# Attention on TensorE: scores from two rounded float32 parts in two 64-row halves, in place of three bfloat16 parts in the whole array

## The reference

```python
x = x + 0.5 * ffn(layernorm(x), ...)
# attention, 16 heads of 16, on y = layernorm(x)
Q = ((y @ W_dq) @ W_uq).reshape(4, 1024, 16, 16)
c = y @ W_dkv
K = (c @ W_uk).reshape(4, 1024, 16, 16)
V = (c @ W_uv).reshape(4, 1024, 16, 16)
scores = einsum('bqhd,bkhd->bhqk', Q, K) / sqrt(16)
attn = softmax(where(causal, scores, -inf))
x = x + einsum('bhqk,bkhd->bqhd', attn, V).reshape(4, 1024, 256) @ W_o
x = x + 0.5 * ffn(layernorm(x), ...)
```

## Time and profile before

| | us |
|---|---|
| median of 3 runs (1258.01 to 1261.18) | 1259.8 |
| span of the profiled execution, first to last instruction | 1263.3 |
| PE busy in it | 1066.7 |
| DVE busy | 829.9 |
| ACT busy | 666.1 |

### The profile page before, as it was taken

How to read it: one execution, slowest core, us unless ns; L and a number is a source line. 1 busy time by engine, 2 the same in 40 slices (tenths; PEclk the granted TensorE clock), 3 DMA queues, 4 the chain that set the end, 5 groups by cost and what they waited for, 6 DMA issues and landing times. The chain is left out here.

```text
span 1263.3 us, 22520 instructions
## 1 busy us (share of the span) xinstructions
PE 1066.7 (84%) x6988; PEld 642.3 (51%) x6988; DVE 829.9 (66%) x2536; ACT 666.1 (53%) x1668; POOL 384.3 (30%) x404
## 2 busy tenths in 40 slices
PE   3539999984988899999999999999859369999940
PEld 2328888872442244443444444444347258888840
DVE  6774444436867888888888888888037754444427
ACT  5605554542753376676777666667636315455520
POOL 6506777752002000000000000000048227777730
PEclk8559999995977699999999999999889759999985
DMA  9503333326756444444444444440057113333339
GB/s 301 186 9 93 101 105 105 102 84 216 201 200 142 59 60 61 61 61 60 61 61 60 60 61 61 61 60 11 10 189 239 58 38 94 104 102 104 105 118 331
DMA packets 109248, 132.53 MB, mean 105 GB/s; under 512 B 29968, under 2 KB 83664, under 8 KB 109136
## 3 DMA queue, kind: packets, MB, share of 16 engines
q1 hardware_dynamic: 91280, 89.65, 31.2%
q0 software_dynamic: 13632, 37.24, 9.3%
q10 hardware_dynamic: 4224, 4.19, 1.0%
HBM read 82.42 MB, written 48.23 MB: 103 GB/s over the span
## 5 line engine op out<-in xcount | busy, mean ns | idle before, releaser
L1415 ACT ACTIVATE stacks_rows_or_prob<-stacks_bank 128x512 f32<-128x512 f32 (+3 forms) x768 | 326.0, 494 | 144.1 <-PE stacks_bank L1347 118.9
L1429 DVE CUSTOM_DVE_ANT_0 stacks_bank<-stacks_bank,all_causal 128x128 f32<-128x128 f32 (+3 forms) x512 | 245.4, 504 | 33.7 <-PE stacks_bank L1318 30.2
L1432 DVE TENSOR_REDUCE t_maxp<-stacks_bank 128x1 f32<-128x512 f32 x256 | 175.5, 686 | 25.0 <-PE stacks_bank L1318 24.4
L1318 PE MATMUL stacks_bank<-stacks_kst,stacks_qst 96*128 96x512 bf16 (+2 forms) x528 | 160.3, 348 | 8.5 <-DVE t_maxp L1429 4.2
L1358 PE MATMUL stacks_bank<-stacks_rows_or_prob,stacks_turned_or_values 128*32 128x512 f32 (+3 forms) x1536 | 164.5, 500 | 3.0 <-ACT stacks_rows_or_prob L1415 1.1
L1344 PE MATMUL stacks_bank<-stacks_qst,stacks_kst 99*128 99x512 bf16 (+3 forms) x528 | 154.9, 335 | 2.5 <-ACT stacks_rows_or_prob L1415 1.9
L1296 POOL COPY stacks_turned_or_values<-stacks_values 128x512 f32<-128x512 f32 x16 | 9.8, 613 | 427.7 <-DMA stacks_kst<-qk_parts 286.5
L1318 PEld LDWEIGHTS stacks_bank<-stacks_kst,stacks_qst 96*128 96x128 bf16 x528 | 48.5, 98 | 126.9 <-DVE t_maxp L1429 66.6
L653 PE MATMUL be_psG<-b_w,be_xT 128*128 x426 | 112.8, 401 | 0.0
L653 PE MATMUL ae_psG<-a_w,ae_xT 128*128 x426 | 111.9, 398 | 0.0
L1347 PE MATMUL stacks_bank<-all_causal_t,all_ident_bf 128*128 128x128 bf16 x512 | 109.6, 221 | 0.0
(11 more groups left out here) (296 smaller groups left out, 1917.7 us busy)
## 6 DMA issues: line engine op xcount, KB each, us to landing
stacks_qst<-qk_parts SPq DMA_DIRECT2D x66, 128.0 KB, 4.9
stacks_kst<-qk_parts SPq DMA_DIRECT2D x66, 128.0 KB, 7.6
stacks_rows_or_prob<-y_rows SPq DMA_DIRECT2D x16, 512.0 KB, 6.1
s_yk<-y_rows SPq DMA_DIRECT2D x16, 512.0 KB, 9.4
stacks_parts_or_stacks<-qk_parts SPq DMA_DIRECT2D x60, 128.0 KB, 6.2
qk_parts<-stacks_parts_or_stacks SPq DMA_DIRECT2D x16, 384.0 KB, 2.6
qk_parts<-q_parts SPq DMA_DIRECT2D x16, 384.0 KB, 3.4
o_rows<-t_orow SPq DMA_DIRECT2D x32, 136.0 KB, 8.7
```

The lines of the kernel that those rows point to most:

```text
L1318: nc.tensor.matmul(psR[bank][:, 0:w], qst[slot][0:KROWS, h, i * P:(i + 1) * P], kst[slot][0:KROWS, h, k0:k0 + w], start=True, stop=True).t ...
L1415: nc.scalar.activation(prob[j % 2][:, h, a:(c + 1) * 512], psS[n % ST_BANKS][:, a - c * 512:512], ACT.Exp, scale=DK ** -0.5).then_inc(exp_ ...
L1429: ins = nc.vector.tensor_tensor_reduce(psR[bank][:, 0:w], psR[bank][:, 0:w], T.causal[:, 512 - w:512], 1.0, -BIG, ALU.add, ALU.max, maxp[: ...
L1432: ins = nc.vector.tensor_reduce(maxp[:, h, col:col + 1], psR[bank][:, 0:w], AX_X, ALU.max)
```

## The change

Q, K and the maxima are kept in two rounded float32 parts (F32R, fp32r) in place of three bfloat16 parts. Three products of parts remain (high times high, high times low, low times high), so a stack has 3 x 16 = 48 rows, 50 with the maxima. Even heads of a group lie in partitions 0 to 63 and odd heads in 64 to 127, so S and T of the two use different 64-row halves of the array; S and T are at least 256 columns wide now (a 128-column piece computes 256). The pieces of S alternate between the two halves, and T's heads do so too. The mask matmul stays as it is. The projections drop `take_high` and `middle`: the high part by ACT, the low one by one DVE subtraction. `split_max` has two operations, `load_max` four DMAs. The rows of ones are written for partitions 32 to 63 and 96 to 127 before the stacks load, and SP waits for that. `plan_step` gives each half a time of its own. The stores of parts grow from 384 to 512 KB each; a group's stack loads remain 12 of 128 KB.

```diff
-PARTS = 3
-Q_PARTS = (0, 0, 0, 1, 1, 2)
-K_PARTS = (0, 1, 2, 0, 1, 0)
+PARTS = 2
+Q_PARTS = (0, 0, 1)
+K_PARTS = (0, 1, 0)
 KROWS = len(Q_PARTS) * DK
 MROWS = KROWS + PARTS
+HALVES = 2
+HALF_ROWS = P // HALVES
+ROUNDED_COLS = 256
...
+    PAIRS = HG // HALVES
+    N_LOADS = HALVES * (len(Q_PARTS) + len(K_PARTS))
...
-        self.qst = [M.sb(f"qst{s}", [P, HG, S], BF16) for s in range(SLOTS - 1)] + [last[0]]
-        self.kst = [M.sb(f"kst{s}", [P, HG, S], BF16) for s in range(SLOTS - 1)] + [last[1]]
+        self.qst = [M.sb(f"qst{s}", [P, self.PAIRS, S], F32R) for s in range(SLOTS - 1)] + [last[0]]
+        self.kst = [M.sb(f"kst{s}", [P, self.PAIRS, S], F32R) for s in range(SLOTS - 1)] + [last[1]]
...
+    def rows(self, st, slot, h, n):
+
+        at = (h % HALVES) * HALF_ROWS
+        return st[slot][at:at + n, h // HALVES, :]
 
     def load(self, sp, g, slot):
         b, hg = g // self.GB, g % self.GB
         for kind, st, which in ((0, self.qst, Q_PARTS), (1, self.kst, K_PARTS)):
             for r, part in enumerate(which):
                 src = self.qk_dram[kind, part, bass.ds(hg * (HG * DK), HG * DK), bass.ds(b * S, S)]
-                sp.dma_start(st[slot][r * DK:(r + 1) * DK, :, :],
-                             src.rearrange("(h d) t -> d h t", d=DK)).then_inc(self.loaded[slot], 16)
+                by_half = src.rearrange("(c a d) t -> a d c t", a=HALVES, d=DK)
+                for a in range(HALVES):
+                    at = a * HALF_ROWS + r * DK
+                    sp.dma_start(st[slot][at:at + DK, :, :].bitcast(F32), by_half[a]).then_inc(self.loaded[slot], 16)
...
+                sp.wait_ge(Q.ones_ready, HALVES * (SLOTS - 1))
...
-                dve.wait_ge(mid_ready, c * NU + u + 1)
-                nc.vector.tensor_tensor(parts[b][:, u, 2, :], bank(c, u)[:], parts[b][:, u, 1, :], ALU.subtract).then_inc(low_ready, 1)
+                dve.wait_ge(high_ready, c * NU + u + 1)
+                nc.vector.tensor_tensor(parts[b][:, u, 1, :], bank(c, u)[:], parts[b][:, u, 0, :], ALU.subtract).then_inc(low_ready, 1)
...
-        def take_high(c, b, u):
-            pe.wait_ge(high_ready, c * NU + u + 1)
-            nc.tensor.matmul(bank(c, u)[:], T.minus_bf[:], parts[b][:, u, 0, :], start=False, stop=True,
-                             skip_group_check=True).then_inc(high_taken, 1)
...
-            take_high(c, b, 0)
+            up(c, b, 2)
             if more:
                 turn(c + 1, 1 - b)
-            take_high(c, b, 1)
-            up(c, b, 2)
             up(c, b, 3)
-            take_high(c, b, 2)
             Q.early_scores(pe, c, 1)
             if more:
                 latents(c + 1, 1 - b)
-            take_high(c, b, 3)
...
-        def middle(c, b, u):
-            act.wait_ge(high_taken, c * NU + u + 1)
-            nc.scalar.copy(parts[b][:, u, 1, :], bank(c, u)[:]).then_inc(mid_ready, 1)
...
-    for h in range(HG):
+    for pair in range(HG // HALVES):
         for i in range(QT):
             end = (i + 1) * P
-            units.append((h, i, 0, min(end, 512), i))
-            if end > 512:
-                units.append((h, i, 512, end - 512, i + QT // 2))
+            for k0 in range(0, end, 512):
+                for a in range(HALVES):
+                    units.append((pair * HALVES + a, i, k0, min(end - k0, 512), i + k0 * QT // (2 * 512)))
...
+            half = half_free[units[u][0] % HALVES] if kind == "s" else max(half_free)
...
+            can.append((max(t, half_free[h % HALVES], st_free[n_st % ST_BANKS], slot_free - 300), had_t / need_t, "t"))
...
-            t = start + w / 2.4
-            dve = max(dve, t + READER_LATENCY) + 64 + (w if kind == "s" else 900) * 1.04
+            end = start + max(w, ROUNDED_COLS) / 2.4
+            if kind == "s":
+                half_free[units[u][0] % HALVES] = end
+                t = start + ISSUE
+            else:
+                half_free = [end] * HALVES
+                t = end
...
-            t = start + (w + P * (max(c * 512, j * P) == j * P)) / 2.4
-            act = max(act, t + READER_LATENCY) + 100 + w * 0.833
+            end = start + max(w, ROUNDED_COLS) / 2.4
+            half_free[h % HALVES] = end
+            t = start + ISSUE
+            if max(c * 512, j * P) == j * P:
+                end = t = max(half_free) + P / 2.4
+                half_free = [end] * HALVES
...
-                sp.dma_start(qst[slot][KROWS + part:KROWS + part + 1, :, :], mparts[:, part, :]).then_inc(m_loaded, 16)
+            wait(sp, drained, max_at(g))
+            for a in range(HALVES):
+                at = a * HALF_ROWS + KROWS
+                rows = slice(a * (MROW // HALVES), (a + 1) * (MROW // HALVES))
+                for part in range(PARTS):
+                    sp.dma_start(qst[slot][at + part:at + part + 1, :, :].bitcast(F32),
+                                 mparts[rows, part, :].bitcast(F32)).then_inc(m_loaded, 16)
...
+    def ones(pool, s):
+
+        for a in range(HALVES):
+            rows = slice(a * HALF_ROWS + HALF_ROWS // 2, (a + 1) * HALF_ROWS)
+            Q.ones_chain.link(nc.gpsimd.memset(kst[s][rows, :, :].bitcast(F32), 1.0))
...
         wait(pe, drained, r + 1 - RING_BANKS)
-        nc.tensor.matmul(psR[bank][:, 0:w], qst[slot][0:KROWS, h, i * P:(i + 1) * P],
-                         kst[slot][0:KROWS, h, k0:k0 + w], start=True, stop=True).then_inc(filled, 1)
+        w = max(w, ROUNDED_COLS)
+        nc.tensor.matmul(psR[bank][:, 0:w], A.rows(qst, slot, h, KROWS)[:, i * P:(i + 1) * P],
+                         A.rows(kst, slot, h, KROWS)[:, k0:k0 + w], start=True, stop=True).then_inc(filled, 1)
 
...
+            wide = min(a, (c + 1) * 512 - ROUNDED_COLS)
             wait(pe, exp_done, g * ST + n + 1 - ST_BANKS)
-            ins = nc.tensor.matmul(ps, kst[k][0:MROWS, h, j * P:(j + 1) * P], qst[k][0:MROWS, h, a:(c + 1) * 512],
-                                   start=True, stop=a > j * P)
+            ins = nc.tensor.matmul(psS[n % ST_BANKS][:, wide - c * 512:512], A.rows(kst, k, h, MROWS)[:, j * P:(j + 1) * P],
+                                   A.rows(qst, k, h, MROWS)[:, wide:(c + 1) * 512], start=True, stop=a > j * P)
             if a == j * P:
                 ins = nc.tensor.matmul(ps[:, 0:P], T.ident_bf[:], T.causal_t[:], start=False, stop=True)
             ins.then_inc(st_done, 1)
...
-            wait(dve, m_loaded, g * (16 * PARTS))
-            nc.vector.tensor_scalar(neg[:], psR[bank][0:MROW, 0:P], -1.0, None, ALU.mult).then_inc(drained, 1)
-            dve.wait_ge(drained, r + 1)
-            link(nc.vector.tensor_copy(mparts[:, 0], neg[:]), g, 2)
-            link(nc.vector.tensor_tensor(mid[:], neg[:], mparts[:, 0], ALU.subtract), g, 3)
-            link(nc.vector.tensor_copy(mparts[:, 1], mid[:]), g, 4)
-            nc.vector.tensor_tensor(mparts[:, 2], mid[:], mparts[:, 1], ALU.subtract).then_inc(m_ready, 1)
+            wait(dve, m_loaded, g * M_LOADS)
+            turned = psR[bank][0:MROW, 0:P]
+            link(nc.vector.tensor_scalar(mparts[:, 0], turned, -1.0, None, ALU.mult), g, 2)
+            nc.vector.scalar_tensor_tensor(mparts[:, 1], turned, -1.0, mparts[:, 0], ALU.mult,
+                                           ALU.subtract).then_inc(drained, 1)
```

More of the change, by code:

```diff
@@ L1145, in plan_step @@
         if n_ring < len(ring):
-            can.append((max(t, ring_free[n_ring % RING_BANKS], joined if ring[n_ring][0] == "m" else 0.0), had_s / need_s, "r"))
+            kind, u = ring[n_ring][:2]
+            half = half_free[units[u][0] % HALVES] if kind == "s" else max(half_free)
+            can.append((max(t, half, ring_free[n_ring % RING_BANKS], joined if kind == "m" else 0.0), had_s / need_s, "r"))
         if n_st < len(st):
@@ L1303, in step @@
                     pool.wait_ge(stored, (Q.CH // 2) * (16 * Q.NU))
-                first.link(nc.gpsimd.memset(kst[SLOTS - 1][KROWS:MROWS, :, :], 1.0))
+                ones(pool, SLOTS - 1)
         def blank(s):
@@ L1426, in row_max @@
         h, i, k0, w, col = units[u]
+        half, pair = h % HALVES, h // HALVES
         dve.wait_ge(filled, r + 1)
@@ L1429, in row_max @@
             ins = nc.vector.tensor_tensor_reduce(psR[bank][:, 0:w], psR[bank][:, 0:w], T.causal[:, 512 - w:512], 1.0, -BIG,
[L1430 removed]
+                                                 ALU.add, ALU.max, maxp[:, half, pair, col:col + 1])
         else:
[L1432 removed]
+            ins = nc.vector.tensor_reduce(maxp[:, half, pair, col:col + 1], psR[bank][:, 0:w], AX_X, ALU.max)
         ins.then_inc(drained, 1)
```

79 lines of the change are left out of this document (39 added, 40 removed).

## The result

The changed kernel takes 1435.9 us (median of 4 runs, 1435.2 to 1436.0 for three of them and 1506.7 for the fourth, which lies outside the comparison) against 1258.9 us: a ratio of 1.142, interval 1.136 to 1.147. It is slower, by more than the 1370 that I forecast. The profiled execution spans 1433.9 us.

A forecast was written before the change was run, and what follows sets the result against it. PE was taken to set the 30.7 us step; streams -4.5 and row-mode changes +11.7 gave 37.9. Fifteen steps +108, the last +5, projections -4: 1259.8 + 109, written 1370 us, range 1280 to 1450.

The forecast's parts named there:

- the named mechanism: PE in the groups: changes between 64-row and 128-row matmuls cost gaps and operand reloads, 11.7 us a group.
- The streams: S and T on PE: 64-row halves side by side take 11.5 us in place of 16.0, gain 4.5 a group.
- the turns of PV and transposes: PE's 128-row work among 64-row S and T: PV reloads +1.2 us, turned maxima and outputs +0.9 us a group.
- The masks' turns: 32 masks a group between 64-row matmuls: 0.10 us out, 0.10 back, 0.10 reload each, +9.6 us a group.
- The step at full clock: One step of a group on PE at 2.4 GHz: 30.7 - 4.5 + 11.7 = 37.9 us, +7.2.
- rival 2: PE's clock falls to 1.2 GHz among the groups: about 56 us a group, about 1660 us in all; chance 0.27.
- third of the time: Milder case of the clock's fall: PE at 1.2 GHz a third of the time, about 1500 us.
- the halting pattern: PE's drains and loads between streams in the groups: the stop-and-go that lowered the clock earlier was said to persist.
- The last step: Last step of the groups, T alone: masked T find no S to pair with, partly covered by ACT's exponentials, +5 us.
- The projections: Projections: PE loses 32 `take_high`, ACT 32 copies, stores grow by a third; -4 us in all.
- Maxima split, memsets, load order: DVE's shorter maxima split, POOL's memsets of ones, and the maxima's and stacks' loads: no effect on the time.
- Rival 1: Gaps on PE are cheap and reloads hide, so DVE binds at 26.7 us a step: about 1194 us; chance 0.18.

The follow-up runs named there:

- b_mask64: Kernel before, each mask matmul replaced by two 64-row matmuls in partitions 0 to 63, other matmuls as they were; 1355.4 us in one run.
- b_rows48: Kernel before with no mask on PE (GpSimd zeroes the weights), bfloat16 S and T over 48 and 50 rows, smaller exponent scale; 1570.8 us, ratio 1.253 to before.
- a_mask64: Changed kernel, each mask matmul replaced by two 64-row matmuls in the half of its own T, same order of work; 1289.4 us in one run.
- a_rows128: Changed kernel with GpSimd masking, rounded float32 S and T over all 128 rows, maxima's loads left out, smaller exponent scale; 1267.8 us, ratio 1.010 to before.
- a_old_split: Changed kernel with `take_high` and `middle` back in the projections, third part into a spare tile that nothing reads; 1544.8 us in one run.
- b_pool_mask: Kernel before with the mask off PE: GpSimd zeroes the masked corner of the weights after the exponential, small exponent scale; 1237.2 us, ratio 0.982.

## Why the prediction was right and wrong

**Slower: right**, and by the named mechanism for half of it. **The time: 66 us short.** 1435.9 lies within my range of 1280 to 1450, but by luck: the range was drawn for pairing and gaps at full clock, and without the clock's share (worked out below) the time would have been about 1347. By its steps:

- The streams (forecast -4.5 us a group) and the turns of PV and transposes (+1.2 and +0.9): -2.4 together. Measured as 30.6 against 30.0, both without masks: +0.6. Mis-sized by 3.0. A few pairs do start together (705.46), others follow each other (706.46). Neither 30.6 nor 30.0 is PE's need alone, so how much of the 3.0 is pairing and how much is turns isn't settled.
- The masks' turns (forecast +9.6): 36.9 - 30.6 = 6.3 us with the masks' own streams, where the kernel before pays 30.7 - 30.0 = 0.7 for its masks. So +5.6. The three times of 0.10 are all in the timeline, but not every turn lengthens the step; b_mask64, with the turns beside full rows, has +6.3 with a second mask piece of up to 1.8 in it. The Trainium skill, "TensorEngine Tiling (Array Packing)", Key Properties, says that a change of mode drains the engine. The trace agrees, with its 0.10 on either side.
- The step at full clock: forecast 37.9, measured 36.9. Two errors of opposite sign made it look good.
- **The step that failed is the clock**, taken as 1.00 in the likeliest case and left to rival 2 (chance 0.27). The fifteen steps at 36.9 would be 553.5 us; they took 629.5, so about 76 us are the clock's. The kernel before has 8.1 of that kind (468.6 less 15 x 30.7), so the clock adds some 68 and the work 93 (15 x 6.2), where I had 108. Rival 2 was right that it falls. Its "third of the time" is what happened (a quarter of each step, all of the first and much of the second and last; a mean of 0.84 over the fifteen), but its "about 1500" doesn't follow from its own terms: a third of the groups at +25 and the rest at +7.2 give about 1470. On why, it named the halting pattern. Halting alone isn't it: b_mask64 has as many turns and is at 1.00. Nor is the share of columns streamed alone: by the prediction's stream times (an estimate) b_mask64 streams some 28 of its 37.0 us, and b_rows48 would stream some 25 of the 32.4 that I expected of it at full clock, the same share, and it fell. But halting seems to have a part where S and T have 64 rows, since a_mask64, without the mask's turns, is mostly at 1.00.
- The last step: forecast +5, measured +26.2. It ran at a mean clock of 0.53; in the kernel before the last step (884.8 to 920.0) is at 0.90. I take the other 21 as the clock's; no run shows that step warm.
- The projections: forecast -4, measured -14.8. 2 to 4 by the split itself at equal clock; the rest goes with a stretch at the lower clock, longer in the profile of the kernel before than in this one, and how much of that the split brings about is open. The stores at DMA share 1.03 cost nothing visible.
- Maxima split, memsets, load order: nothing to see, as forecast.

In sum the spans differ by 170.6 for the 109 forecast: some +89 for the clock (68 and 21), -15 for the work of the steps, -12.5 for projections and experts.

Rival 1 (gaps cheap, 1194) fails twice: the turns cost, and when they are taken away a step of 30.6 is still PE's. Its gain wasn't to be had in this order.

Why 64-row matmuls hold the clock less well isn't shown; that they do is, by b_rows48 and a_rows128 and by every trace of the set. The Trainium skill, "TensorE: Matmul & The Clock Gate", Part 1, has the clock follow how busy TensorE is. The profile's count of busy time doesn't bear that out here: PE counts as busy for all 60.00 us of b_rows48's window at 0.50 and for 29.84 of 30.00 in a_rows128's at 1.00.

## What to carry to other kernels

Before packing two small matmuls into row halves, count the full-row operations between them (masks, transposes, products of weights): each costs about 0.2 us of a PE-bound step, and a pair has to save more. Look at the clock row of the page before any share: a_rows128 and b_rows48, both with PE near 100%, differed by a factor of 1.6 a step, and half rows side by side lost to full rows one after another. A 128x128 mask costs 0.29 us on an idle GpSimd, and a step was no longer for it; taken off PE it was worth 1.8% to the kernel before, though for a kernel with the reference's scale the exponential must first be kept from overflowing in masked entries, which wasn't tried.

## What the runs showed of the hardware

- A step with one fixed instruction stream had two stable courses, 61.1 us at 1.2 GHz throughout and 41.0 us with 10.3 of them at 1.2 GHz, and one execution (a_old_split) went from the first to the second by itself.
- With bfloat16 S and T over 48 and 50 rows TensorE was at 1.2 GHz in all fifteen steps, 51.6 us each (b_rows48); over 96 and 99 rows it was at 2.4 GHz, 30.0 us each (b_pool_mask).
- Rounded float32 over 128 rows stayed at 2.4 GHz from 420 to 889 us, 32.3 us a step (a_rows128).
- Changing between 128-row and 64-row matmuls left a gap of 0.10 us each way at 2.4 GHz (changed kernel, 703.09 to 703.56; b_mask64, 605.84 to 606.37).
- GpSimd's 32 selects a group (9.7 us of its time) left VectorE's time in a group as it was: 27.0 us in 30.0, for 27.2 in 30.7.
